# Blocks of sorted tokens at four slots each, their second bias added by VectorE, and three loads at a layer border moved earlier

## The reference, cut to what matters

```python
router_probs = softmax(xt @ Wr + br)
gates = max(router_probs); idx = argmax(router_probs)
h = relu(xn @ W1[idx] + b1[idx])          # 128 -> 512
y = (h @ W2[idx] + b2[idx]) * gates       # 512 -> 128
```

## Time and profile before

| | |
|---|---|
| median of 3 runs | 694.93 us (692.76 to 696.48) |
| the profiled execution: its own time | 695.81 us |
| its span, from the first to the last instruction | 694.0 us |
| PE, DVE, POOL, ACT busy | 84%, 83%, 77%, 66% |
| layer 0 and its setup | to about 258 us of the span |
| layer 1 | from about 258 us to the end |

### The profile page before, as it was taken

How to read it: one execution, slowest core, us unless ns; L and a number is a source line. 1 busy time by engine, 2 the same in 40 slices (tenths; PEclk the granted TensorE clock), 3 DMA queues, 4 the chain that set the end, 5 groups by cost and what they waited for, 6 DMA issues and landing times. The chain is left out here.

```text
span 694.0 us, 8481 instructions
## 1 busy us (share of the span) xinstructions
PE 585.4 (84%) x2135; PEld 339.7 (49%) x2135; DVE 575.8 (83%) x906; ACT 456.4 (66%) x723; POOL 532.7 (77%) x431
## 2 busy tenths in 40 slices
PE   4656888899745966889999799998799999899997
PEld 2412667786413423544444454444454544566674
DVE  6899819677788987997988979888989788898995
ACT  4655466877834666856787655886765887776660
POOL 3456356785785575988899799999799999799991
PEclk9999899999877988999999999999999999999999
DMA  8096896898796677677557686767676867678870
GB/s 267 17 322 229 291 296 207 286 288 294 218 306 238 224 193 183 177 201 189 153 158 198 177 203 198 189 160 190 175 197 185 208 168 192 173 204 215 221 197 15
DMA packets 71216, 142.25 MB, mean 205 GB/s; under 512 B 8352, under 2 KB 37088, under 8 KB 71168
## 3 DMA queue, kind: packets, MB, share of 16 engines
q1 hardware_dynamic: 67984, 130.74, 66.6%
q0 software_dynamic: 3184, 10.98, 4.7%
HBM read 133.23 MB, written 8.45 MB: 204 GB/s over the span
## 5 line engine op out<-in xcount | busy, mean ns | idle before, releaser
L927 DVE TENSOR_TENSOR_SCAN state<-decay,bank 128x512 f32<-128x512 f32 x128 | 155.9, 1218 | 12.9 <-POOL product L1262 5.3
L2019 PE MATMUL bank<-xw,wu 128*128 128x512 f32 x256 | 133.9, 605 | 14.3 <-DVE hid L1046 11.0
L1262 POOL TENSOR_TENSOR product<-state,CB 128x512 f32<-128x512 f32 x90 | 117.0, 1300 | 16.1 <-DVE state L927 12.3
L1264 POOL TENSOR_TENSOR product<-product 128x512 f32<-128x512 f32 x90 | 119.5, 1328 | 7.1
L1671 ACT ACTIVATE sg<-bank 128x512 f32<-128x512 f32 x128 | 75.4, 597 | 67.4 <-PE bank L1909 58.8
L2037 PE MATMUL bank<-hid,wd 128*128 128x512 f32 x192 | 99.1, 597 | 7.2 <-DVE hid L1046 7.2
L1046 DVE TENSOR_TENSOR hid<-sg,bank 128x512 f32<-128x512 f32 x128 | 85.0, 666 | 22.3 <-PE bank L2019 20.6
L920 DVE TENSOR_TENSOR bank<-bank,CB 128x512 f32<-128x512 f32 x128 | 88.8, 694 | 13.4 <-DMA CB<-crow 11.5
L1921 PE MATMUL bank<-product,early 128*128 128x512 f32 x112 | 71.3, 737 | 32.8 <-POOL product L1307 13.5
L1583 ACT ACTIVATE decay<-delta,negA 128x510 f32<-128x510 f32 x128 | 82.5, 710 | 12.0 <-DVE delta L885 6.8
L1907 PE MATMUL bank<-XH,wh 128*128 128x512 f32 x128 | 74.1, 579 | 9.9 <-ACT sg L1671 3.6
(11 more groups left out here) (242 smaller groups left out, 1137.3 us busy)
## 6 DMA issues: line engine op xcount, KB each, us to landing
CB<-crow SPq DMA_DIRECT2D x256, 256.0 KB, 4.1
CB<-crow SPq DMA_DIRECT2D x44, 512.0 KB
cwb<-cwrow SPq DMA_DIRECT2D x32, 256.0 KB, 4.7
szm<-crow SPq DMA_DIRECT2D x11, 512.0 KB
cwb<-crow SPq DMA_DIRECT2D x9, 512.0 KB
xw<-Wg_dram SPq DMA_DIRECT2D x8, 256.0 KB, 2.9
wd<-Wd_dram SPq DMA_DIRECT2D x8, 256.0 KB, 5.5
wu<-Wu_dram SPq DMA_DIRECT2D x8, 256.0 KB, 5.3
```

The lines of the kernel that those rows point to most:

```text
L927: v.tensor_tensor_scan(state[:, c % RING, :], decay[:, PLACE[c], :], drive, 0.0, ALU.mult, ALU.add).then_inc(state_ready.sem, 1)
L1262: p.tensor_tensor(addend, state[:, c % RING, :], cs, ALU.mult).then_inc(state_used.sem, 1)
L1264: ins = p.tensor_tensor(product[:, m, :], product[:, m, :], addend, ALU.add)
L2019: t.matmul(bank[up_bank(i, u)][:, :], wu[:, e, 128 * f:128 * f + 128], xw[:, e % 2, :], start=True, stop=True).then_inc(up_ps.sem, 1)
```

## The change

Two things change. First the blocks: DVE takes a block out of PSUM and adds the second bias with it, in slot +5, and the bias matmuls go away. Blocks go at four slots each, the last three at three. POOL loads a pack in slot -5 and waits for the take of the block three before, which now reads the pack too. The last block keeps its slots, except that its take is one later.

Second the border: SP issues `load_x(1)` in slot 110 and both `load_cw` in slot 119, ahead of the eight loads of rows.

```diff
+NEXT_X_AT, FIRST_CW_AT = 14, 23
-UP_AT = [20 + 3 * b if b < 4 else 17 + 4 * b for b in range(BLOCKS)]
+UP_AT = [20 + 4 * b if b < 12 else 31 + 3 * b for b in range(BLOCKS)]
 TURN_AT, TURN_IN_AT = [at - 2 for at in UP_AT], [at - 1 for at in UP_AT]
-RELU_AT, DOWN_AT, TAKE_AT = ([at + lag for at in UP_AT] for lag in (1, 3, 4))
-PACK_AT, LOAD_AT = ([at + lag for at in UP_AT] for lag in (-6, -5))
+RELU_AT, DOWN_AT, TAKE_AT = ([at + lag for at in UP_AT] for lag in (1, 3, 5))
+PACK_AT, LOAD_AT = ([at + lag for at in UP_AT] for lag in (-5, -5))
...
                 if s == GATED_AT[0] + 5:
                     load_x(0)
+                if s == 3 * UNITS + NEXT_X_AT:
+                    load_x(1)
+                if s == 3 * UNITS + FIRST_CW_AT:
+                    load_cw(0, 0)
+                    load_cw(0, 1)
...
-                if i == 0:
-                    load_cw(0, 0)
-                    load_x(1)
-                    load_cw(0, 1)
...
+                for b in now(TAKE_AT, s):
+                    take_out(b)
...
+            def take_out(b):
+                dve.wait_ge(blk_down.sem, blk_down.at0(0, b + 1))
+                if b >= 2:
+                    dve.wait_ge(blk_out_done[b % 2].sem, blk_out_done[b % 2].at0(0, 16 * (b // 2)))
+                b2 = pack[:, b % PACKS, PACK_COLS - D:PACK_COLS].rearrange("p (a d) -> p a d", a=1).to_broadcast((128, 2, D))
+                src = bank[OUT_BANK][:, 0:BLOCK].rearrange("p (k d) -> p k d", k=2)
+                v.tensor_tensor(blk_out[:, b % 2, :, :], src, b2, ALU.add).then_inc(blk_out_ready.sem, 1)
...
                 if b >= PACKS:
-                    pool.wait_ge(blk_down.sem, blk_down.at0(0, b - PACKS + 1))
+                    pool.wait_ge(blk_out_ready.sem, blk_out_ready.at0(0, b - PACKS + 1))
...
-            def take_out(b):
-                act.wait_ge(blk_down.sem, blk_down.at0(0, b + 1))
-                if b >= 2:
-                    act.wait_ge(blk_out_done[b % 2].sem, blk_out_done[b % 2].at0(0, 16 * (b // 2)))
-                a.activation(blk_out[:, b % 2, :, :], bank[OUT_BANK][:, 0:BLOCK].rearrange("p (k d) -> p k d", k=2), ACT.Copy).then_inc(blk_out_ready.sem, 1)
...
-                        t.matmul(dst, blk_h[:, b % 2, f, 128 * k:128 * k + 128], pack[:, b % PACKS, at:at + D], start=(f == 0), stop=False)
-                    last = t.matmul(dst, top_row[:, :], pack[:, b % PACKS, PACK_COLS - D:PACK_COLS], start=False, stop=True)
+                        last = t.matmul(dst, blk_h[:, b % 2, f, 128 * k:128 * k + 128], pack[:, b % PACKS, at:at + D], start=(f == 0), stop=(f == FT - 1))
```

More of the change, by code:

```diff
@@ L1630, in slot0 @@
                     tail(k, name)
-                for b in now(TAKE_AT, s):
-                    take_out(b)
                 for b in now(RELU_AT, s):
```

## The result

The changed kernel took 686.44 us (median of 4 runs, 684.94 to 688.05) against 695.7 us (692.76 to 697.93) for the kernel before on the same chip: ratio 0.9877 [0.9845, 0.9909]. The ratio is that of 686.44 to 694.93 us, the median of three of these four runs, 8.5 us; the gap of the two medians given here is 9.3. The profiled execution took 684.94 us, with a span of 683.2.

What follows compares the result with a forecast made beforehand. The prediction saw no engine busy throughout; the first four blocks ran as a chain at 7.2 us each. Blocks -6.2 and border -2.8 gave -9.0 us, from the median 694.93 to 686 us; range 678 to 695 us.

Steps and rivals of the forecast that it cites:

- A: Whole kernel: both parts, blocks and border, pay, giving 681 to 690 us; chance 0.47.
- The chain at the start: First blocks of layer 0: 5.7 us a block against 7.2, DVE's first split_low near 89.3 instead of 96.46; -7.0 us.
- The bias matmuls: Blocks of layer 0: removing them frees PE of 0.44 us a block, counted in ten of 15; -4.4 us.
- Given back: Layer 0: three blocks instead of four start before slot 34; the fourth costs time later, at the last three; +3.7 us.
- The take on DVE: Blocks of layer 0: 0.42 us each on DVE, covered by its idle time; its waits for PE cost +1.5 us.
- Rival E: Blocks of layer 0: DVE's waits at the takes put scans in series with PE's sums; slower, 699 to 705 us; chance 0.14.
- The border: Between layers 0 and 1: earlier cw and token loads save 3.6 us and cost 0.8; -2.8 us, bounds -6.6 and +1.
- the price of the late rows: At the border: two more issues and 0.5 MB ahead of the first row loads delay the first drive; cost 0 to 2.5 us.
- a microsecond gained or lost at its start should reach the end: Layer 1: POOL, PE and DVE are near their limit in a fixed order, busy 101.13, 99.69 and 96.90 of 110 us.
- POOL and DVE together at the border: POOL's weighing now runs while DVE adds two SBUF tensors, which may hold some up; cost 0 to 1 us.
- by the rule alone: At the border, POOL sharing its SBUF way with DVE makes the sum one POOL instruction worse, some -2.3 us.
- Rival D: Blocks of layer 0: DMA, 0.96 busy at 310 GB/s, takes back PE's gain; no change, 692 to 696 us; chance 0.12.

Runs made afterwards that it cites:

- e11: Kernel before with the slots where ACT rounds the gate weights and DVE forms the rest, and SP's later gate weight loads, eight later: 695.41 us, ratio 1.0015.
- e5: Changed kernel with the two bias matmuls of each block kept on PE, DVE taking the block as a plain copy: 687.28 us, ratio 0.9897.
- e9: Changed kernel with the three gaps of three slots between blocks spread apart instead of all at the end: 685.97 us, ratio 0.9875.
- e3: Kernel before with only the new pace of the blocks; copy stays on ACT, bias on PE: 688.97 us, ratio 0.9923.
- e10: Changed kernel with DVE's take one slot later, three slots behind the down product: 683.92 us, ratio 0.9853.
- e8: Changed kernel with the take doubled: DVE adds the bias within PSUM, then copies the block to SBUF: 686.21 us, ratio 0.9892.
- e2: Changed kernel with the three border loads left where they were before, so the blocks' change alone: 686.71 us, ratio 0.9895.
- e4: Changed kernel's take on DVE with the second bias, but the old pace and the old border loads: 688.45 us, ratio 0.9915.
- after: The changed kernel itself, with all edits, against the kernel before: 686.44 us, ratio 0.9877.
- e1: Kernel before with only the three border loads moved: 694.67 us, ratio 0.9997.
- e12: Changed kernel with ACT taking the blocks by a plain copy in the same slot, second bias left out altogether: 683.48 us, ratio 0.9834.
- e6: Changed kernel with the two loads of layer 1's first row pair issued ahead of the two cw loads: 686.36 us, ratio 0.9885.
- e7: Changed kernel with only the second pair's tokens loaded early, both cw loads behind the eight row loads: 686.6 us, ratio 0.9901.

## Why the prediction was right, step by step

**The whole**: 686.0 was forecast, 686.44 measured; the case was A, and faster than 0.5%. The blocks were to give 6.2 us and give 7.3 (4.4 to 10.2) alone. The border was to give 2.8 and gives 0.2 within 1.7 alone. So the sum is that close partly by luck. The border's error is clear of the noise. What makes up for it, the blocks giving more than forecast, is within the noise.

**The chain at the start, -7.0**: right, and the best-read part. The first blocks were to follow each other at 5.7 us; their takes are 5.5 and 5.8 us apart (77.30, 82.75, 88.59), and `split_low` is at 89.53 for 89.3. That the 10.80 us on DVE only show the chain was argued, and e11 shows it. What was wrong is the cause given: taking the copy from ACT is not needed. The pace alone gives 5.4 us with ACT's takes in place, and cuts ACT's waits at the first of them from 12.3 to 4.7 us; the take and bias alone give 5.9 at the old pace. Either edit loosens the chain of transposing, relu, down, bias and take; the terms were added where by the traces they overlap.

**The bias matmuls, -4.4**: mis-sized as a term of this sum. e5 gives 1.4 us. The step that failed is "where PE is full", taken as ten blocks of 15. Only one window of the kernel before bears it out, that from 140 to 160 us. In the two ahead of it PE has room:

```profile
100.00:120.00 20.00, 16.71 (x94) 13.65 (x93) 15.18 (x27) 14.73 (x31) 11.80 (x10) 0.94 0.65 218
120.00:140.00 20.00, 18.00 (x102) 14.69 (x102) 13.92 (x15) 15.61 (x30) 15.33 (x14) 0.93 0.90 287
```

At the new pace the full window goes too: PE is busy 17.96 us of it, and 17.67 with the bias kept (e5). So 0.44 us a block is partly idle time of PE.

**Given back, +3.7**: the direction is right, the size is not shown. The scans stand 10.2 us ahead of before at slot 37, 9.0 at slot 67, 11.4 at slot 69 alone, 7.6 at slot 71 and 8.0 at the end of layer 0 (counted from the first scan 0.4 more each), so about 2 us go. Where it lands was said to be "the three-slot pace of the last three blocks"; e9 spread them and kept no more of the lead (7.2 us at the end, 8.4 in the changed kernel, both from the first scan). What goes with the last scan is the last take: in every kernel but e9 the lead of the one over before is that of the other within 1.4 us (e3: 7.4 and 6.8; e10: 9.9 and 9.9). The last take was forecast near 171 and came at 168.90. After the blocks DVE is busy 19.15 of 20 us, so what comes early there queues on DVE; that this is the whole cause was not tested.

**The take on DVE, 0 for its work and +1.5 for its waits**: the work is covered (e8, 6.4 us more of it, no loss), at 415 ns against 0.42 us. The waits cost about what was booked: a slot more of distance returns 1.7 us by the ratios, which is not certain. Rival E had the waits right (12.5 us, three of them over 2) and their price wrong; that the sums have slack behind their scans, which would explain it, was argued and not tested.

**The border, -3.6 + 0.8**: this failed, in two terms. First the base: the earlier trace rows are one execution in which the stretch from the last scan of layer 0 to the ninth of layer 1 took 38.6 us; four others with the same order of loads (e2, e3, e4, e11) took 37.9, 36.7, 36.9 and 36.9. With the new order it is 35.9 to 37.2 in seven (after, e1, e5, e8, e9, e10, e12), 36.6 in the mean, against 37.4: -0.8 us. Second, the price of the late rows, 0 to 2.5 with little booked: 1.69 and 3.14 us of waiting at the first drive. That wait is no loss of its own either, as e6 shows, where it goes and the 73rd scan stays at 36.3. "DVE saves its 4.04 us" treated a wait as a gain, though the next thing DVE needed was as late: counted from the last scan of layer 0, `stat1` comes at 13.4 to 14.6 us in the seven and at 14.7 to 15.8 in the five with the old order, and the third scan of layer 1 at 18.2 to 19.4 against 18.9 to 20.1. PE's 3.2 us did arrive at its first up (12.6 to 13.6 against 15.3 to 16.3), but the layer did not keep them: "a microsecond gained or lost at its start should reach the end" does not hold for one gained on PE alone. Why not was not tested.

**POOL and DVE together at the border, 0 to 1**: line 887, named in the prediction by its old number 885, took 0.68 us, as before. The next one, line 893, took 1.48 us where line 891 had taken 0.70, while POOL ran line 1382: 0.8 us, inside the 0 to 1; the 0.8 booked was for this and the late rows together. (The sum "by the rule alone", some -2.3 us, doesn't follow from its terms: one POOL instruction of 1.1 us more is -1.7, or -2.5 if it takes the place of the 0.8.) The take, with one input in PSUM, ran at 77.30 and at 82.75 us beside POOL products (76.55 and 82.14, 1.27 and 1.28 us long) and took 0.42 us both times, no more than without one. The rule of the Trainium skill that POOL shares its way to SBUF with DVE instructions that have two SBUF inputs (GPSIMD Engine Reference, Specifications) agrees with both.

**Rival D**: at the start the DMA engines reached 0.97 and 337 GB/s, above the 310 it took as the rate, and no long wait for rows came. It fell.

## What to carry to other kernels

A long wait on one engine is worth only what the next thing it needs allows: ask for each wait you remove what its engine will need next and when that arrives, and move the wait on paper first (e11: 10.80 us became 9.65; the border: 4.04 became 1.69 to 3.14). Two edits that break the same chain must be priced together, and a term priced by an engine's fullness must be priced at its fullness after the other edits. Before pricing a hole of a few us, compare the same stretch in several executions; here one lay 1.5 us above the mean of four others, half of the 2.8 that was forecast.

## What was not expected of the hardware

The four kernels that are alike up to slot 109 took 200.9 to 204.0 us for that stretch and what follows to the last scan of layer 0, and the granted clock does not order them: e6, the shortest, had 0.970 in the mean of its span, e2 (201.9 us) the lowest, 0.938, e7, the longest, 0.960.

Where POOL and DVE meet, the loser seems to wait rather than to run slower: POOL's line 1382 went from 250.91 to 252.01, DVE's line 893 started at 251.08 and ended at 252.56, 0.55 us behind POOL, when alone it takes 0.70. POOL's next one, begun at 252.16, took 1.35 us in place of 1.10. Which of them loses goes by who starts first: in e5 POOL did, in e12, where the same instruction is line 1371, DVE.

```profile
252.59 1.10 POOL L1382 TENSOR_TENSOR xw<-XNP,cwb 128x512 f32<-128x512 f32 x1 [1.00 <-DMA cwb<-cwrow]
252.77 1.48 DVE L893 TENSOR_TENSOR bank<-delta,xs 128x512 f32<-128x512 f32 x1
```

```profile
249.50 0.70 DVE L893 TENSOR_TENSOR bank<-delta,xs 128x512 f32<-128x512 f32 x1
249.63 1.52 POOL L1371 TENSOR_TENSOR xw<-XNP,cwb 128x512 f32<-128x512 f32 x1 [1.32 <-DMA cwb<-cwrow]
```

The Trainium skill says so (SBUF — State Buffer, Terms: the shared port pair is exclusive and held for the full instruction, and the loser blocks fully). These rows agree: the loser ends 0.55 to 0.95 us behind the winner, its own time alone less some 0.15 us.
